# First batch's keys and queries asked for at the projection's last product, in a place of their own

## The reference

```python
q = einsum('bsd,ed->bse', x, Wq).reshape(bsz, seqlen, HQ, D)
k = einsum('bsd,ed->bse', x, Wk).reshape(bsz, seqlen, HK, D)
v = einsum('bsd,ed->bse', x, Wv).reshape(bsz, seqlen, HK, D)
q, k = _rope(_rmsnorm(q, q_norm_w), pos), _rope(_rmsnorm(k, k_norm_w), pos)
kc = k_cache[block_table].reshape(bsz, L, HK, D)
vc = v_cache[block_table].reshape(bsz, L, HK, D)
k_all, v_all = concatenate([kc, k], axis=1), concatenate([vc, v], axis=1)
scores = einsum('bqhd,bkhd->bhqk', q, k_all) * SCALE
probs = softmax(where(valid, scores, -1e30))
o = einsum('bhqk,bkhd->bqhd', probs, v_all)
return einsum('bse,de->bsd', o, Wo)
```

## Time and profile before

| | us |
|---|---|
| median of three runs | 2404.17 |
| lowest, highest | 2403.21, 2405.09 |
| profiled execution, its own time | 2405.73 |
| span of the profiled execution | 2403.6 |
| TensorE busy (matmuls) | 2279.4, 95% of the span |
| VectorE, ScalarE, GpSimd busy | 1793.8, 1302.3, 1167.9 |
| mean DMA rate over the span | 209 GB/s |

### The profile page before, as it was taken

How to read it: one execution, slowest core, us unless ns; L and a number is a source line. 1 busy time by engine, 2 the same in 40 slices (tenths; PEclk the granted TensorE clock), 3 DMA queues, 4 the chain that set the end, 5 groups by cost and what they waited for, 6 DMA issues and landing times. The chain is left out here.

```text
span 2403.6 us, 52557 instructions
## 1 busy us (share of the span) xinstructions
PE 2279.4 (95%) x16384; PEld 1970.0 (82%) x16384; DVE 1793.8 (75%) x3555; ACT 1302.3 (54%) x2627; POOL 1167.9 (49%) x1246
## 2 busy tenths in 40 slices
PE   4869899999998599999999999999999997999999
PEld 4858677777776599999999999999999997788887
DVE  6654399999998588888888888888888886432221
ACT  2652588888887355555555555555555554421111
POOL 3420144444444477767777677777767774000000
PEclk7989999999999799999999999999999999999999
DMA  5563333333322788888888888888888885743442
GB/s 224 204 214 99 88 110 108 97 103 109 109 88 83 234 295 294 292 294 276 285 292 291 288 295 289 278 292 293 292 291 294 276 285 185 248 123 101 127 140 61
DMA packets 451704, 501.65 MB, mean 209 GB/s; under 512 B 95653, under 2 KB 390565, under 8 KB 443302
## 3 DMA queue, kind: packets, MB, share of 16 engines
q1 hardware_dynamic: 414758, 366.37, 47.6%
q0 software_dynamic: 36864, 134.23, 15.9%
HBM read 404.02 MB, written 96.47 MB: 208 GB/s over the span
## 5 line engine op out<-in xcount | busy, mean ns | idle before, releaser
L1103 POOL TENSOR_TENSOR att_probs<-att_probs,att_inverse 128x512 f32<-128x512 f32 x512 | 535.3, 1046 | 290.0 <-DVE att_inverse L1299 285.6
L1207 ACT ACTIVATE att_probs<-att_probs,att_low 128x544 f32<-128x544 f32 x512 | 383.8, 750 | 515.6 <-DVE att_low L1286 448.4
L1164 PE MATMUL att_o<-att_probs_t,att_values 128*128 128x128 f32 x4096 | 540.9, 275 | 0.0
L1286 DVE CUSTOM_DVE_ANT_0 att_probs<-att_score,att_mask,att_batch_cols 128x544 f32<-128x544 f32 x512 | 399.6, 780 | 140.0 <-PE att_score L1129 100.7
L1164 PEld LDWEIGHTS att_o<-att_probs_t,att_values 128*128 128x128 f32 x4096 | 497.7, 192 | 0.0
L1295 DVE COPY att_probs_t<-att_turn 128x512 f32<-128x512 f32 x512 | 350.4, 684 | 1.2 <-PE att_turn L1144 1.2
L1089 POOL DMA_INDIRECT att_values<-L_cond_v_cache,att_v_rows_of x256 | 282.2, 1103 | 82.4 <-POOL att_v_rows_of L1085 49.9
L1129 PE MATMUL att_score<-att_keys_raw,att_queries_raw 128*128 128x288 f32 (+1 forms) x1024 | 290.9, 407 | 28.9 <-DMA att_queries_raw<-q_t 26.7
L1144 PE MATMUL att_turn<-ident,att_probs 128*128 128x128 f32 x2048 | 311.3, 275 | 1.2 <-POOL att_probs L1103 0.8
L798 PE MATMUL proj_proj<-x3t_hi,proj_w_hi 128*128 128x512 f32 x640 | 266.9, 417 | 6.9 <-DVE proj_w_lo L858 6.9
L1144 PEld LDWEIGHTS att_turn<-ident,att_probs 128*128 128x128 f32 x2048 | 244.3, 141 | 32.9 <-POOL att_probs L1103 1.4
(11 more groups left out here) (128 smaller groups left out, 3986.8 us busy)
## 6 DMA issues: line engine op xcount, KB each, us to landing
att_keys_raw<-L_cond_k_cache SPq DMA_DIRECT2D x1024, 128.0 KB
q_t<-proj_q_out SPq DMA_DIRECT2D x32, 1024.0 KB, 3.9
att_queries_raw<-q_t SPq DMA_DIRECT2D x64, 512.0 KB
o_t<-att_heads_out SPq DMA_DIRECT2D x64, 512.0 KB, 6.5
out_o_raw<-o_t SPq DMA_DIRECT2D x32, 1024.0 KB, 5.7
front_adapters<-L_cond_weight SPq DMA_DIRECT2D x16, 1024.0 KB, 10.9
w_nat<-L_cond_Wq SPq DMA_DIRECT2D x8, 1024.0 KB, 5.3
v_new<-values_v_out SPq DMA_DIRECT2D x64, 128.0 KB, 2.0
```

Source lines behind the costliest of these rows:

```text
L1103: nc.gpsimd.tensor_tensor(probs[:, k, 0:L], probs[:, k, 0:L], inverse[:, k:k + 1].to_broadcast([P, L]), ALU.mult).then_inc(probs_ready, 1)
L1164: last = nc.tensor.matmul(o, values[j][:, t, h * D:(h + 1) * D], probs_t[m % 2][:, t * P:(t + 1) * P], start=(t == 0), stop=False, skip_gr ...
L1207: nc.scalar.activation(probs[:, k, :], probs[:, k, :], ACT.Exp, bias=low[k][:, 0:1], scale=-1.0, accum_out=total[k][:, 0:1]).then_inc(exp_ ...
L1286: nc.vector.tensor_tensor_reduce(out=probs[:, k, :], in0=score_ps[:, LEFT:LEFT + KEYS], in1=mask[j][:], scale=batch_cols[j][:, h:h + 1], s ...
```

## The change

The first batch's keys and queries get tiles of their own, `keys_first` and `queries_first`. Their place (21 KB of each partition) is fixed ahead of the projection's tiles, given back at once, and then covered by the transposed rows `x3t_hi` during the projection; attention reserves the same place (`keys_home`, `queries_home`) and uses these tiles as its buffers of number 0. They can thus be written once the projection's last product is done. SyncE asks for them in the last chunk of the last head, in `first_keys`: it waits for the page numbers, for the earlier stores that used the same buffers (which also hold the first batch's queries and keys), and for `proj_done` to reach the last product. Ten pages, the new keys and the queries go ahead of the chunk's two stores, six pages behind them. The first batch's page numbers have a small load and a clamp of their own at the projection's start. In attention, SyncE's wait for all page numbers moves behind the load of the first new values, and it loads only the second batch there.

```diff
+        EARLY = 10
+        first_pages = a_.sb("first_pages", [1, NPP], I32)
...
                 for rc in range(RC):
+                    if last and rc == RC - 1:
+                        pages = first_keys()
                     sp.wait_ge(rotated, h * TPH + (rc + 1) * M)
                     sp.dma_start(qt_dram[bass.ds(h, 1), :, rc * CB:(rc + 1) * CB, :].rearrange("h d b n -> d (h b n)"),
                                  q_out[rc % 2].rearrange("d b r s -> d (b r s)")).then_inc(q_stored[rc % 2], 16)
                     sp.wait_ge(k_scaled, h * RC + (rc + 1))
                     sp.dma_start(kn_dram[rc * CB:(rc + 1) * CB, :, bass.ds(h, 1), :].rearrange("b d h s -> d b (h s)"),
                                  k_out[rc % 2][:]).then_inc(k_stored[rc % 2], 16)
-
+                    if last and rc == RC - 1:
+                        load_pages(pages, range(EARLY, NPP))
+
+            def load_pages(pages, which):
+                for n in which:
+                    sp.dma_start(keys_first[:, n], kt[bass.ds(pages[n], 1)].rearrange("n d h k -> d (n h) k")).then_inc(keys_loaded[0], 16)
+
+            def first_keys():
+
+                sp.wait_ge(pages_ready, 1)
+                _, pages = nc.values_load_multi_w_load_instructions(
+                    first_pages[0:1, :], engines=(mybir.EngineType.SP,), min_val=0, max_val=PAGES - 1,
+                    skip_runtime_bounds_check_because="VectorE has put every page number between 0 and PAGES - 1")
+                sp.wait_ge(q_stored[0], 16 * HK * (RC // 2))
+                sp.wait_ge(k_stored[0], 16 * HK * (RC // 2))
+                sp.wait_ge(proj_done, HK * TPH)
+                load_pages(pages, range(EARLY))
+                sp.dma_start(keys_first[:, NPP], kn_dram[0:1].rearrange("b d h s -> d (b h) s")).then_inc(keys_loaded[0], 16)
+                sp.dma_start(queries_first[:], qt_dram[:, :, 0:1, :].rearrange("h d b n -> d h (b n)")).then_inc(keys_loaded[0], 16)
+                return pages
+
+            sp.dma_start(first_pages[:], table[0:1, :]).then_inc(pages_loaded, 16)
             heads(sp, head)
...
             for m in range(M):
                 split_weights(0, 0, m)
+            dve.wait_ge(pages_loaded, 16)
+            nc.vector.tensor_scalar(first_pages[:], first_pages[:], 0, PAGES - 1, ALU.max, ALU.min).then_inc(pages_ready, 1)
             heads(dve, head)
...
+        a_.sb("keys_home", [P, NPP + 1, HK, PSIZE])
+        a_.sb("queries_home", [P, HK, P])
+        keys_raw = [keys_first, a_.sb("keys_raw1", [P, NPP + 1, HK, PSIZE])]
+        queries_raw = [queries_first, a_.sb("queries_raw1", [P, HK, P])]
         pages_sb = a_.sb("pages", [1, B * NPP], I32)
-        keys_raw = [a_.sb(f"keys_raw{v}", [P, NPP + 1, HK, PSIZE]) for v in range(2)]
-        queries_raw = [a_.sb(f"queries_raw{v}", [P, HK, P]) for v in range(2)]
...
             sp.dma_start(pages_sb[:], table.rearrange("(o b) n -> o (b n)", o=1)).then_inc(pages_loaded, 16)
-            sp.wait_ge(pages_ready, 1)
...
-            load_keys(0, 0, 0, True)
             load_new_values(0, 0, 0, True)
+            sp.wait_ge(pages_ready, 1)
             load_keys(1, 1, 0, True)
             load_new_values(1, 1, 0, True)
...
+            keys_loaded = [ctx.enter_context(nc.semaphore(f"keys_loaded{v}")) for v in range(2)]
+            with (nc.sbuf_tensor("keys_first", [P, NPP + 1, HK, PSIZE], F32) as keys_first,
+                  nc.sbuf_tensor("queries_first", [P, HK, P], F32) as queries_first):
+                pass
```

More of the change, by code:

```diff
@@ L686, in load_head_weights, with stage_projection @@
     sp.dma_start(w_nat[:, 1:, :], wq[bass.ds(h, 1)].rearrange("h p m c e -> p (h m) (c e)")).then_inc(loaded, 16)
-def stage_projection(nc, wq, wk, ident, x3t_hi, x3t_lo, rope, w_nat, stat, qt_dram, kn_dram):
+def stage_projection(nc, wq, wk, ident, x3t_hi, x3t_lo, rope, w_nat, stat, qt_dram, kn_dram,
+                     table, kt, keys_first, queries_first, keys_loaded):
     with ExitStack() as ctx:
@@ L717, in stage_projection @@
         w_loaded = a_.sem("w_loaded")
+        pages_loaded = a_.sem("pages_loaded")
+        pages_ready = a_.sem("pages_ready")
         w_hi_ready = a_.sem("w_hi_ready")
@@ L945, in _, with stage_attention @@
             heads(pool, head)
-def stage_attention(nc, table, v_cache, ident, stat, v_index, kt, kn_dram, qt_dram, vn_dram, ot_dram):
+def stage_attention(nc, table, v_cache, ident, stat, v_index, kt, kn_dram, qt_dram, vn_dram, ot_dram,
+                    keys_first, queries_first, keys_loaded):
     N = 2 * HK
@@ L998, in stage_attention @@
         pages_ready = a_.sem("pages_ready")
-        keys_loaded = a_.sem("keys_loaded", 2)
         hi_ready = a_.sem("hi_ready")
@@ L1563, in program @@
                              x3t_dram, vn_dram)
-                stage_projection(nc, wq, wk, ident, x3t_hi, x3t_lo, rope, w_nat, stat, qt_dram, kn_dram)
-            stage_attention(nc, table, vc, ident, stat, v_index, kc, kn_dram, qt_dram, vn_dram, ot_dram)
+                stage_projection(nc, wq, wk, ident, x3t_hi, x3t_lo, rope, w_nat, stat, qt_dram, kn_dram,
+                                 table, kc, keys_first, queries_first, keys_loaded)
+            stage_attention(nc, table, vc, ident, stat, v_index, kc, kn_dram, qt_dram, vn_dram, ot_dram,
+                            keys_first, queries_first, keys_loaded)
         stage_output(nc, wo, ident, ot_dram, x3_dram, out.rearrange("b s t -> (b s) t"))
```

## The result

The changed kernel takes 2395.89 us, the median of ten runs, beside 2403.48 for the kernel before, also of ten. The medians differ by 7.6 us. The ratio, which counts all runs and not the middle ones alone, is 0.9972, with a 95% interval of 0.9962 to 0.9981: 6.7 us less on 2403.48, from 4.6 to 9.1. Two more series on other chips gave 0.9965 (0.9951 to 0.9979) and 0.9967 (0.9954 to 0.9980), with medians 9.8 and 10.6 us apart. The change is faster beyond its interval, but by the first ratio by little more than half of the 12.6 us that I forecast. Put on the 2404.17 from which I counted, that ratio gives 2397.4, just outside my range of 2389.0 to 2396.5 (the median 2395.89 itself lies inside it). The profiled execution took 2394.80 us, with a span of 2392.8.

What follows compares the result with a forecast made beforehand. Attention was taken to run at TensorE's pace, DMA close behind, after a 26.7 us gap. A 13.5 us gain at the first scores less 0.9 for the second batch gave 12.6 less: 2391.6 us, range 2389.0 to 2396.5.

Steps and rivals of the forecast that it cites:

- Where the gain lies and what bounds it: Attention runs at TensorE's pace, its loop untouched; starting it earlier shortens the 26.7 us TensorE gap before its first scores.
- neither clamp nor small load: At the projection's start, the added 1x16 load and VectorE clamp cost nothing, or 0.7 us if VectorE's idle cover were gone.
- The failed step: At the projection's end, stores held behind loads put the key store's landing at 787.0 and attention's start at 787.5, 3.7 us later.
- The order in which the stores wait for the loads: On SyncE's queue at the projection's end, stores wait for bytes of loads asked for earlier, moving the boundary by 3.7 us.
- 13.5: At attention's start, VectorE takes the first scores at 792.9 instead of 806.42, a gain of 13.5 us.
- the second batch's lateness: In attention, ScalarE's first split waits 3.0 us for the second batch's keys, landing at 809.3; loss 0.9 us (0 to 2.3).
- hidden by 1 to 3 us: In attention's first batch, gathered values land at 799.6 to 801.6, before TensorE needs them at 802.8.
- The starting point: One profiled execution before the change, span 2403.6 and time 2405.73 us, with times counted on the three-run median 2404.17.
- Stores beside loads: Rival at the projection's end: stores run beside loads, boundary at 784.0, 14.5 us gained, 2389.7 us; chance 0.12.
- The second batch taking it back: Rival in attention: transfers collide, second batch's keys land at 814, 5.6 us lost, 7.9 gained, 2396.3 us; chance 0.20.
- the clock stays low: Rival in attention: TensorE stays at its lower clock, each further step costs 0.9 us, 2409 us; chance 0.03.

Runs made afterwards that it cites:

- queries last: First batch's queries asked for behind the six late pages instead of ahead of the two stores, against the changed kernel; ratio to before 0.9955 (0.9942 to 0.9968).
- the page numbers early: Changed kernel with the second batch's page numbers in the early small table, its keys asked for before the clamp; ratio to before 0.9952 (0.9939 to 0.9966).
- the three edits: Changed kernel with last stores on ScalarE's queue, second batch's page numbers early, VectorE's mask and splits before its clamp; 2390.46 us, ratio to before 0.9943.

## Why the prediction was right and wrong

*Where the gain lies and what bounds it: right.* The loop is unchanged, and nothing outside the stretch from the last product to the 17th masking differs. TensorE's gap fell from 26.7 to 13.4 us (forecast about 12), ScalarE waited 3.0 us for the second batch, TensorE 1.0, each as worked out. The clock did not stay low, and the projection's last product came no later than before, so neither clamp nor small load shows a cost.

*The failed step: "The key store lands 0.7 us after its last byte, as before, at 787.0, and attention begins at 787.5, 3.7 us later than now."* Counted from the last product that is 14.3 us; three profiles had 16.3 to 16.6, so the boundary moved by 5.9 us and not by 3.7. Of the 2.0 us in the first profile 1.1 are the key store's landing (14.9 us, forecast 13.8) and 0.9 are SyncE, which ended after it. The order in which the stores wait for the loads was right, and the last experiment on the queue shows it. Two sizes in it were wrong. The queries ahead of the stores cost 2.3 to 2.5 us where I put 1.6 (0.52 MB at 332 GB/s). I took a mean rate over keys, values and queries together for one transfer in pieces of 512 bytes, and the DMA rates of the changed kernel from 777 to 784 us, in slices of 0.175 us, dip where the queries are:

```profile
GB/s 334 199 182 205 146 246 386 293 258 258 211 263 240 111 240 348 211 82 32 29 41 61 181 231 249 275 336 331 348 538 357 571 307 614 328 468 562 234 515 281
```

Five slices, from 780.0 to 780.8, are under 90 GB/s just after the queries and the stores were issued. The other two profiles dip there as well (to 44 and 73 GB/s); in `queries last`, where the queries were not yet asked for, the slices from 779 to 782.6 stay at 100 or more. That the queries make the dip is the likely reading, not a measured one. I also read the query store's bytes in the earlier trace rows as ending at 781.2, where they end at 781.0; read so, my key store lands 0.2 us earlier and the miss is that much larger. And SyncE, which I costed at 0.57 us a page, was held 5.29 us by one page behind the key store; it ended 0.9 us after that store's landing, so the boundary waited for the issue and not for the landing. By my cost SyncE would have been done with the six pages at 784.7, 2.3 us before that landing, so I took the landing alone for the boundary. The trace of before had a row that pointed there and that I passed over, the issue behind the first queries:

```profile
797.48 2.02 SPq L1047 DMA_DIRECT2D att_new_values<-v_new  x1
```

One 128 KB load took SyncE 2.02 us right behind a transfer in small pieces; a page behind other pages takes 0.57. But small pieces just ahead are not enough: in the changed kernel the query store went out right behind the same kind of transfer in 0.58 us, and the hold came two issues later. The holds grew with what was queued (3.64 us without the queries ahead, 5.3 to 6.0 with them); whether the number of pieces, their bytes or something else sets them, no run here shows. The first masking was thereby 21.3 us after the last product rather than 19.7, and 11.4 us of gain came of 13.5 (32.7 less 21.3, on the means of three).

*A term mis-sized: the second batch's lateness.* From the first to the 9th masking the means are 21.1 and 22.7 us, a loss of 1.6 where I had 0.9. From the sixth to the ninth, where the second batch's keys are first split, they are 7.4 and 9.3 us, so all of it arises there, and the page numbers early brought it back to 7.3. The keys were asked for 20.1 us after the last product, forecast 18.4, since the boundary was late. The clock's return is no part of the mean loss (11.5 us after the first score matmul before, 11.2 after), though it moves single profiles. In one of three profiles TensorE also waited 0.8 us for the first values, which I had called hidden by 1 to 3 us: they are not, in every execution.

*The starting point.* I took one profile of before as the rule. Its stretch was 73.4 us where the mean is 72.7. By terms: 13.5 - 0.9 = 12.6 forecast; 11.4 - 1.6 = 9.8 in the profiles, the measured 9.7 but for rounding.

*What stays open.* The three series of runs give 6.7, 8.4 and 7.9 us by their ratios, 7.6, 9.8 and 10.6 by their medians, and the profiled executions 9.7. The intervals reach to 9.1, 11.8 and 11.1, so the last two allow it. In each series some executions of the changed kernel are 4 to 10 us longer than its fastest (up to 2400.16 and 2402.89); none of the three profiled ones was such an execution, so what is long in them isn't known. The kernel before spreads too (2399.62 to 2406.77 in the first series), so some of the 3 us between 6.7 and 9.7 may be chance.

*The rivals.* Stores beside loads was wrong: on one queue the stores waited for the loads, and even on a queue of its own the key store landed 6.3 us after issue, against 3.0 before. The second batch taking it back was the right direction, and too large: of the missing gain up to the 17th masking 1.6 us were lost by the boundary and 0.7 by the second batch. That the clock stays low did not happen: it returned 11.8, 11.3 and 10.5 us after the first score matmul, before 12.1, 9.9 and 12.5.

## What to carry to other kernels

A load moved ahead of a stage's last stores on the same queue delays them by its own transfer, and the stage boundary with them; count it at the rate of its own piece size, and put what has small pieces behind the stores or on another queue. When a transfer of many small pieces is queued behind others, the next issue can hold the whole issuing engine (3.6 to 6.0 us here), so what it issues next, and the end of its stage, are late as well. When a gap is halved, look at once for what was hidden in it: here the clamp on VectorE and the second batch's keys, which together with the stores were worth another 5 us at the 17th masking (one profile). And take a stretch from several executions before a difference of some microseconds is forecast from it.

## What the runs showed of the hardware

SyncE's issue of a 128 KB page took 0.50 us with nothing but pages ahead (5.01 for ten) and 0.80 on average behind the queries and a 1 MB store in large pieces (4.82 for six, the longest 1.55). The first page behind a 256 KB store in pieces of 128 bytes took 5.29, 5.55 and 5.42 us with the queries ahead of the stores, and 3.64 without them. Two queues did not shield each other: with the stores on ScalarE's, SyncE's new keys and queries took 1.23 and 1.40 us to issue instead of 0.43 (1.49 and 1.05 with the three edits). TensorE's granted clock fell to 0.50 some 0.5 to 1.3 us after its last matmul of the projection and came back 9.9 to 14.2 us after the first score matmul, in three executions of the kernel before up to 2.6 us apart. These are the two windows of half a microsecond before and at its return in the changed kernel:

```profile
801.00:801.50 0.50, 0.50 (x2) 0.36 (x3) 0.50 (x2) 0.50 (x2) 0.00 (x0) 0.50 1.05 377
801.50:802.00 0.50, 0.50 (x4) 0.42 (x3) 0.50 (x2) 0.11 (x2) 0.00 (x0) 0.89 1.03 363
```
